# Second attention of a two-layer kernel: whole value products, two a turn, and the difference's product first

## The reference

```python
glo = jnp.mean(mixed_q, axis=1, keepdims=True)
c = jnp.tanh(mixed_q @ wfq + bfq + (glo @ wfg + bfg))
...
P = jax.nn.sigmoid(p) * key_len
Z = jax.nn.sigmoid(z) * key_len
G = -(j[None, None, None, :] - P[..., None]) ** 2 * 2.0 / Z[..., None] ** 2
scores = jnp.einsum('bhqd,bhkd->bhqk', q, k) / jnp.sqrt(jnp.float32(D))
scores = scores + G
probs = jax.nn.softmax(scores, axis=-1)
ctx = jnp.einsum('bhqk,bhkd->bhqd', probs, v)
```

## Time and profile before

| what | us |
|---|---|
| median of three runs | 1718.99 |
| the profiled execution, own time | 1718.05 |
| its span, first to last instruction | 1716.1 |
| PE busy over the span | 1604.8 (94%) |
| VectorE busy | 1224.8 (71%) |
| ScalarE busy | 1074.3 (63%) |
| GpSimd busy | 764.2 (45%) |
| mean granted TensorE clock | 0.958 |

### The profile page before, as it was taken

One profiled execution on the slowest core, in us unless ns is written; L12 is line 12 of the kernel. 1 busy time (PEld: TensorE's weight loads), 2 busy tenths in 40 slices (PEclk: granted clock), 3 DMA queues, 4 the chain that ended last, 5 costly groups with the idle time before them and its releaser, 6 DMA issues. The chain is left out here.

```text
span 1716.1 us, 32583 instructions
## 1 busy us (share of the span) xinstructions
PE 1604.8 (94%) x12584; PEld 510.4 (30%) x12584; DVE 1224.8 (71%) x2620; ACT 1074.3 (63%) x1325; POOL 764.2 (45%) x467
## 2 busy tenths in 40 slices
PE   7899999999999999998699859999999999999996
PEld 3232333323232333322244412222222222222232
DVE  6767666675757666661467466889889898888965
ACT  2444554545454544444365436999999999998984
POOL 3577788878788788889224223000300030000012
PEclk8999999999999999999799865999999999999998
DMA  5000000000000000000202460111211122111000
GB/s 117 32 14 14 8 14 14 7 20 8 14 13 14 7 14 13 8 19 7 35 3 58 99 144 1 25 26 25 43 25 25 25 51 37 29 26 25 2 2 25
DMA packets 76509, 46.87 MB, mean 27 GB/s; under 512 B 22271, under 2 KB 75203, under 8 KB 76355
## 3 DMA queue, kind: packets, MB, share of 16 engines
q1 hardware_dynamic: 75010, 43.55, 12.2%
q10 hardware_dynamic: 1344, 1.25, 0.2%
HBM read 25.66 MB, written 9.31 MB: 20 GB/s over the span
## 5 line engine op out<-in xcount | busy, mean ns | idle before, releaser
L1762 ACT ACTIVATE probs<-ps_e 128x1024 f32<-128x1024 f32 x512 | 522.6, 1025 | 61.2 <-PE ps_e L1862 43.3
L369 POOL TENSOR_TENSOR acc<-acc,probs 128x1024 f32<-128x1024 f32 (+3 forms) x256 | 503.3, 1966 | 77.5 <-ACT probs L422 55.9
L422 ACT ACTIVATE probs<-ps_e 128x1024 f32<-128x1024 f32 (+1 forms) x320 | 285.9, 902 | 370.9 <-PE ps_e L591 123.5
L1999 DVE TENSOR_REDUCE maxpart<-ps_r 128x1 f32<-128x512 f32 x722 | 454.2, 683 | 47.4 <-PE ps_r L1834 47.4
L1872 PE MATMUL ps_o<-probs,v 128*9 128x256 f32 (+1 forms) x3952 | 314.1, 390 | 1.3 <-ACT probs L1762 1.3
L1834 PE MATMUL ps_r<-krows,qrows 60*128 60x512 bf16 x873 | 291.4, 396 | 20.7 <-DVE identb L1965 19.2
L608 PE MATMUL ps_o<-probs,v 128*64 128x512 f32 (+3 forms) x1280 | 307.4, 559 | 0.2 <-ACT pv_raw L429 0.2
L1862 PE MATMUL ps_e<-qrows,krows 62*128 62x512 bf16 x1024 | 298.4, 385 | 1.5 <-DMA qrows<-maxrow 0.9
L698 DVE TENSOR_REDUCE maxpart<-ps_x 128x2 f32<-128x1024 f32 x192 | 234.5, 1221 | 74.7 <-PE ps_x L516 74.7
L1695 POOL TENSOR_SCALAR nrows<-krows 60x4096 bf16<-60x4096 bf16 x3 | 31.6, 10549 | 323.4 <-DMA krows<-k_rows 323.3
L701 DVE CUSTOM_DVE_ANT_0 masked<-ps_x,later 128x128 f32<-128x128 f32 (+3 forms) x256 | 115.0, 486 | 61.3 <-PE ps_x L516 60.2
(11 more groups left out here) (319 smaller groups left out, 1676.1 us busy)
## 6 DMA issues: line engine op xcount, KB each, us to landing
qrows<-q_rows SPq DMA_DIRECT2D x64, 192.0 KB
rbc<-rden SPq DMA_DIRECT2D x128, 64.0 KB, 2.1
q_rows<-parts_q SPq DMA_DIRECT2D x24, 128.0 KB, 2.4
k_rows<-parts_k SPq DMA_DIRECT2D x24, 128.0 KB, 2.4
krows<-k_rows SPq DMA_DIRECT2D x16, 192.0 KB, 5.5
w_rows<-parts_w SPq DMA_DIRECT2D x6, 256.0 KB, 2.3
qrows<-a_rows SPq DMA_DIRECT2D x64, 24.0 KB
qrows<-w_rows SPq DMA_DIRECT2D x64, 24.0 KB
```

The costliest lines, as they stand in the source:

```text
L369: pool.tensor_tensor(acc[:, u % 2, :, o:], acc[:, u % 2, :, o:], probs[:, turn % RING, :, o:], ALU.add)\
L422: act.activation(probs[:, turn % RING, :, o:], ps_e[:, turn % 2, :, o:], ACT.Exp, scale=1.0 / math.sqrt(D0))\
L1762: act.activation(probs[:, HG * (turn % 2) + hh], ps_e[:, e % 2], ACT.Exp).then_inc(s_ex, 1)
L1999: dve.reduce_max(maxpart[:, at:at + 1], ps_r[:, k, :], AX.X).then_inc(s_bf[k], 1)
```

## The change

A turn's value products become two whole ones of 512 queries, one behind the scores of heads 0 and 1 and one behind those of heads 2 and 3. The order of the blocks is now 0, 3, 2, 4, 6, 1, 5, 7: the difference first, before any scores of the turn, and block 1, which joins it, sixth. ScalarE takes the positive part before the turn's exponentials instead of behind the first one. "fin" and "mt" go to the end of their turn, in the banks' order and on PE.

```diff
--- before.py
+++ after.py
@@ -1611,7 +1611,7 @@
             if turn < 0:
                 return [("max", b) for b in range(BU + LEAD)]
             first = BU + LEAD * (turn + 1)
-            return [("max", first + n) for n in (0, 3, 2, 1, 4, 5, 6, 7) if first < NU * BU]
+            return [("max", first + n) for n in (0, 3, 2, 4, 6, 1, 5, 7) if first < NU * BU]
 
         def plan():
 
@@ -1629,7 +1629,7 @@
                 if turn < 0:
                     turns.append([place(op) for op in ops[:BU + 1]] + [place(op) for op in extra] + [place(op) for op in ops[BU + 1:]])
                 else:
-                    turns.append([place(op) for op in ops[:2]] + [place(op, bank) for op in extra] + [place(op) for op in ops[2:]])
+                    turns.append([place(op) for op in ops] + [place(op, bank) for op in extra])
             end = place(("fin", NU - 1), 2)
             steps = {key: place(("step", *key), n % 2)[3:] for n, key in enumerate(STEPS)}
             return turns, end, steps
@@ -1803,11 +1803,11 @@
                     weights_out(n // 8 - 1)
             for turn in range(NU * TU):
                 u, at = divmod(turn, TU)
+                for op in TURNS[turn]:
+                    if op[0] == "max" and op[1] in DIFF:
+                        positive(op[1])
                 for hh in range(HG):
                     exps(HG * turn + hh)
-                    for op in TURNS[turn][2 * hh:2 * hh + 2]:
-                        if op[0] == "max" and op[1] in DIFF:
-                            positive(op[1])
                 if at == 0 and u > 0:
                     copy_pv(u - 1)
             copy_pv(NU - 1)
@@ -1863,28 +1863,18 @@
                                    qrows[64 * j:64 * j + R_END, u % 3, at * P // KB, hh, :], start=True, stop=True)
                 mm.then_inc(s_st, 1)
 
-            def pv(turn, j, first, last):
+            def pv(turn, j):
+                if turn < 0:
+                    return
                 u, at = divmod(turn, TU)
                 pe.wait_ge(s_ex, HG * turn + HG)
                 if at == 0 and j == 0 and u > 0:
                     pe.wait_ge(s_oc, u)
                 for hh in range(HG):
-                    mm = pe.matmul(ps_o[32 * hh:32 * hh + D1 + 1, first:last], v1[:, TU * j + at, HG * (u // NQ) + hh, :],
-                                   probs[:, HG * (turn % 2) + hh, j, first:last], start=at == 0 and j == 0,
+                    mm = pe.matmul(ps_o[32 * hh:32 * hh + D1 + 1, :], v1[:, TU * j + at, HG * (u // NQ) + hh, :],
+                                   probs[:, HG * (turn % 2) + hh, j, :], start=at == 0 and j == 0,
                                    stop=at == TU - 1 and j == 1, skip_group_check=True)
-                if last == QC:
-                    mm.then_inc(s_pv, 1)
-
-            def pv_part(turn, hh):
-                if turn < 0:
-                    return
-                if turn % TU == 0:
-                    if hh == 1:
-                        pv(turn, 0, 0, QC)
-                    elif hh > 1:
-                        pv(turn, 1, QC // 2 * (hh - 2), QC // 2 * (hh - 1))
-                else:
-                    pv(turn, hh // 2, QC // 2 * (hh % 2), QC // 2 * (hh % 2 + 1))
+                mm.then_inc(s_pv, 1)
 
             def weight_step(n):
                 if n == 0:
@@ -1936,24 +1926,36 @@
                     weight_step(n // 8 - 1)
             pe.wait_ge(s_lc, 7)
             for turn, ops in enumerate(TURNS):
-                rest = list(ops)
-                for hh in range(HG):
-                    scores(turn, hh)
-                    for op in rest[:1]:
+                special = [op for op in ops if op[0] != "max"]
+                blocks = [op for op in ops if op[0] == "max"]
+                closing = [PE_SLOT[turn % TU, hh] for hh in (1, 3) if turn >= (NU - 1) * TU and (turn % TU, hh) in PE_SLOT]
+
+                def maxima(first, last):
+                    for op in blocks[first:last]:
                         ring(op)
-                    pv_part(turn - 1, hh)
-                    for op in rest[1:2]:
-                        ring(op)
-                    rest = rest[2:]
-                    if turn >= (NU - 1) * TU and (turn % TU, hh) in PE_SLOT:
-                        step(*PE_SLOT[turn % TU, hh])
-                for op in rest:
+
+                maxima(0, 2)
+                scores(turn, 0)
+                scores(turn, 1)
+                maxima(2, 4)
+                pv(turn - 1, 0)
+                for key in closing[:1]:
+                    step(*key)
+                maxima(4, 6)
+                scores(turn, 2)
+                maxima(6, 7)
+                scores(turn, 3)
+                pv(turn - 1, 1)
+                maxima(7, 8)
+                for op in special:
                     ring(op)
+                for key in closing[1:]:
+                    step(*key)
                 if turn == (NU - 1) * TU - 1:
                     step("ct", 0)
                     step("ct", 1)
             for j in range(2):
-                pv(NU * TU - 1, j, 0, QC)
+                pv(NU * TU - 1, j)
             ring(LAST)
             for kind in ("ct", "wo", "xt", "ff"):
                 step(kind, NQ - 1)
```

## The result

The changed kernel takes 1788.12 us (median of four runs, 1787.98 to 1788.16), the kernel before 1719.6 in the same comparison: a ratio of 1.0399, 95% interval 1.0387 to 1.0412. That is slower by 68.5 us, on the side that was forecast, but beyond the range: 1759 was forecast, 1782 was its upper end.

A forecast was written before the change was run, and what follows sets the result against it. PE was taken to bound the second attention; turns -12, boundary waits +36, fifteenth boundary +0.3, clock +17 and last unit -1.5 summed to +40 us on 1718.05, forecast 1759 us as median, range 1733 to 1782.

The forecast's parts named there:

- clock: After boundary idles the granted clock falls to half speed at 12 of 14 boundaries, 1.4 us each, +17 us.
- wait at the boundaries: At unit ends the scores wait for the late transpose's DMA: 3.7 us against 1.1 before, +36 us for 14.
- turns, "fin", last unit: Second attention's turns -12 us over 119, "fin" 0, last unit without maxima -1.5 us.
- 3.3 us at half speed lose 1.65, less 0.25 ... 1.4 each: Behind a boundary stall, PE's 3.3 us low stretch loses 1.65, waits take in 0.25, leaving 1.4 us each.
- +30 if each lasts longer: Upper bound of the clock term, +30 us instead of +17, if each low stretch at a boundary lasts longer.
- first rival: The clock stays up behind the boundary idles, 17 us less: 1742 us; chance 0.22.
- The fifteenth boundary: Turn 119, without blocks: PE waited 1.85 us for maxhl before, two steps stand behind it; +0.3 us.
- The ordinary turn: Second attention's turn taken as 4.58 us, 0.10 less than 4.68 before; PE's own sum 4.55, bounds 4.50 and 4.72.
- at most 0.1 us, and the pause before head 3 takes it in: Block 4's ring wait for the positive part, in the difference's bank, is at most 0.1 us and absorbed before head 3.
- fin: "fin" moves within its turn and keeps its four transposes: 0, or half a microsecond per unit either way.
- turns get longer: Rival: turns take 4.72 us, 119 x 0.14 = +17, 1776 us, likewise if low stretches last longer; chance 0.13.
- The one on the faster side: Rival: changes of shape cost nothing, VectorE bounds at 4.3 us a turn, 45 us gained, 1709 us; chance 0.04.

The follow-up runs named there:

- filled: Changed kernel with three thrown-away whole f32 products in front of each unit's first scores, inside the DMA wait; 1754.46 us, ratio 1.021.
- mt_early: Changed kernel with the transpose of the maxima back behind the turn's first two blocks, "fin" still at the end; 1711.41 us, ratio 0.9957 to the kernel before.
- half_both: Against mt_early: block 7 reduced over every second key and the positive part taken over every second key; 1698.38 us, ratio 0.9881.
- late_only: Kernel before with only "mt" and "fin" moved to the end of their turn, half products and old order kept; 1792.74 us, ratio 1.0428.
- mt_third_fin: Against mt_early: transpose one block later, behind three blocks, and in the last unit "fin" before its turn's first value product; 1707.54 us, ratio 0.9933.
- seven_first: Against mt_early: block 7 in front of the turn's second value product instead of behind it; 1727.41 us, ratio 1.0049.

## Why the prediction was wrong

Its mechanism was right and is shown by taking it out (76.7 us) and by doing it, with the late "fin", to the kernel before (74.0 us): the transpose at the end of turn 7 puts a DMA's landing in front of the next unit's scores, and the clock falls behind the idle. What failed is sizes. The forecast of +40 and the measured +68.5, term by term:

| term | forecast | measured | from |
|---|---|---|---|
| clock | +17 | +33.7 | changed kernel less filled |
| wait at the boundaries | +36 | +43.1 | filled less mt_early |
| turns, "fin", last unit | -13.5 | -7.4 | mt_early less before |

The three measured terms add to 69.4; they come from two comparisons.

**The clock** was the largest miss, and the step that failed is "3.3 us at half speed lose 1.65, less 0.25 ... 1.4 each", for 12 of 14 boundaries. All 14 fell, and the low stretch at each was 6.8 us, about twice the 3.3 us that I read from two places before the second attention. Two more low stretches of 3.4 us stand at the fifteenth boundary (1720.7) and in the last unit (1737.7). By ScalarE's timeline the changed kernel needs 31.8 us more than filled up to the start of the last unit, 2.3 for each of 14 boundaries where 1.4 was forecast, and 3.0 more in the last unit, where nothing was; its second attention begins 1.2 us earlier, which makes the 33.7 of the medians. At the first boundary PE worked in 5.5 us of the low stretch and lost about half of that, less its slack: ScalarE's timeline has turn 0 at 7.1 us instead of 4.94 in the filled kernel. I had "+30 if each lasts longer" as a bound and did not carry it into the likeliest sum; the range's upper end took in only 6 us of it. The two low stretches in the earlier trace rows were of equal length, and both of one kind: PE was back before the clock fell (at 64.66 and 797.73, low from 64.80 and 798.70). At the 14 boundaries of the changed kernel it fell while PE was still idle, and of that kind all stretches are the long ones (last section). What the first rival made of the case, a clock that stays up, is excluded by every boundary.

The Trainium skill, page "TensorE: Matmul & The Clock Gate", section "HAM oscillation", has the pattern: a wait for a DMA in every tile, and every tile starts slow. The trace agrees, at each boundary without exception.

**The wait** was forecast as 3.7 us a boundary, 2.6 more than the 1.1 of before. The 1.1 is turn 7 alone; turn 0 takes 4.96 us, so a boundary cost 1.4 before. In the filled kernel the two turns at a boundary take 8.68 and 4.94 us, 4.3 over two ordinary ones; in mt_early the same two are 1.4 over. So +2.9 each. From A, the start of head 3's scores in turn 7 (1094.72), the transpose comes at A + 1.83 where A + 1.60 was forecast, the issue at A + 2.78 (A + 2.54), the scores at A + 5.98 (A + 5.47). The first 0.23 are one round more in front of the value product. In an ordinary turn block 5 has run ahead of head 3, and head 3's two products run side by side. Here block 5 waited for a bank that VectorE, held up by rowmax and maxhl, gave back late (PE's weight load for it waits 0.49 us for maxpart). So it started beside head 3's first product, and the second had a round of its own. The landing varied: 3.20 us from issue to scores here, 2.89 at the boundary of 1230 us, 2.75 to 3.42 over the 14, 2.93 in my sum. The fifteenth boundary, forecast at +0.3, costs 2.2 in the filled kernel against mt_early (40.35 and 38.20 us for unit 14): I had counted on PE's wait for maxhl going away, and the steps behind it did not cover the landing.

**The ordinary turn** was forecast at 4.58 and is 4.65. The step that failed is "at most 0.1 us, and the pause before head 3 takes it in". The ring's wait of block 4 lies in the stretch between the second value product and the first (2.69 us in the rows above, 2.59 by my sum), the pause of head 3 in the other (1.95 us, as summed). PE is in order and nothing behind block 4 has a reserve, so 0.1 us stays 0.1 us: 119 x 0.07 = 8 us. half_both puts it at 4.57, so the sum itself was right.

**"fin"** was put at nothing and gained: turns 2 and 3 took 1237.52 - 1227.22 = 10.30 us before (positive part to positive part on ScalarE) and 9.77 after (1245.63 to 1255.40). In 15 units that is some 7 us, and it hid the turn's miss; that the two misses nearly cancel is luck. In late_only, with the old order, the late "fin" takes only 0.26 us off the two turns; no run moved it alone in the new order, so how the rest divides is open. In the last unit it is the other way round: VectorE's copies and norms stand behind "fin", PE's next steps behind them, and moving it to the turn's end costs the 2.0 us that mt_third_fin gets back.

The rival "turns get longer" did not come true, though its other half, low stretches that last longer, did. The one on the faster side did not come true either: each change of PE's shape costs its 0.09 us in the after trace too (0.32 from block 7 to the difference, 0.32 on to block 3).

## What to carry to other kernels

When a hand-off through a DMA is moved, count from its issue to its consumer how much of the slowest engine's work is left between them; here 2.8 to 3.4 us must be covered, and two places that both cover it cost the same to the hundredth of a microsecond (39.16 us a unit with the transpose behind two or three blocks), the next one later did not. An idle of some 3 us in this PE-bound loop cost nearly twice itself (2.9 us of wait and 2.3 of low clock a boundary), because PE came back at half speed; price the low stretch by its longest, not by two examples. In a loop with a small ring of buffers, change the size of the long steps and the order of the short ones together, and try either alone: one of them may be a loss that the other turns.

## What the runs showed of the hardware that was not expected

- Behind an idle of 2.9 us at the first boundary, with 0.4 us of work before it and 0.29 us of idle before that, the granted clock was 0.50 from 1099.5 to 1106.2, although PE was busy without a gap from 1100.70 on. The same length came at the first 14 boundaries of the changed kernel.
- The low stretch at a boundary has two lengths. In late_only both occur; two of its boundaries in the busy time by stretch:

```profile
1101.10:1107.80 6.70, 5.69 (x35) 0.86 (x35) 2.34 (x5) 3.17 (x4) 0.00 (x0) 0.50 0.79 146
...
1237.60:1240.90 3.30, 3.30 (x23) 0.49 (x21) 1.13 (x2) 2.22 (x3) 0.00 (x0) 0.50 1.06 175
1241.10:1246.00 4.90, 4.90 (x46) 1.09 (x44) 4.33 (x8) 4.35 (x7) 0.00 (x0) 1.00 1.00 176
```

  and the start of the scores at the second in PE's timeline:

```profile
1237.30 0.39 PE L1862 MATMUL ps_e<-qrows,krows 62*128 62x512 bf16 x2 [3.92 <-DMA qrows<-maxrow]
```

  At the first boundary the clock fell about 1101.05, while PE was still idle (its scores start at 1102.11, in the row shown in the section on that kernel), and stayed low 6.8 us. At the second it fell about 1237.58, when PE was back since 1237.30, and stayed low 3.4 us. Seven boundaries of this kernel are of the one kind and seven of the other, the first 14 of the changed kernel are of the first (the fall about 1099.45, the scores at 1100.70), its fifteenth is of the second (PE back at 1720.13, the fall about 1720.7, 3.4 us low), and no boundary of the two traces is an exception.
- The same holds at a place in the first attention that no edit touched, behind the idle of 1.91 us of the earlier trace rows. In ten of the twelve traces, the kernel before among them, the clock fell there while PE worked, and was low 3.4 us. In late_only it fell at 66.81, in a gap of 0.22 us, and was low 6.8 us; seven_first has the same. PE's row behind that gap:

```profile
66.97 0.61 PE L516 MATMUL ps_x<-k_hi,q_hi 64*128 64x512 f16 x2 [0.22 <-DVE maxpart L701]
```

  That is a regularity of these traces; no run here set the moment of the fall, so it is not shown as a cause.
- The same idle does not always bring a fall. The idle of 2.82 to 2.85 us ahead of the product at 797.73 of the earlier trace rows is in all twelve traces; behind it the granted clock fell in four, the kernel before among them, and stayed at 1.00 in eight, the changed kernel among them.
- Adding 2.7 us of products that nobody reads, at each of 15 boundaries, made a kernel 33.7 us faster.
